# A fused RWKV layer on one core: powers of two 16x16 blocks streamed as 16 columns, with a new order of the engines' work

## The reference

```
def step(s, inp):
    q_, w_, k_, v_, a_, b_ = inp
    sa = jnp.einsum('bhij,bhj->bhi', s, a_)
    s = s * w_[:, :, None, :] + sa[..., None] * b_[:, :, None, :] + v_[..., None] * k_[:, :, None, :]
    return (s, jnp.einsum('bhij,bhj->bhi', s, q_))
...
_, y = jax.lax.scan(step, s0, (qt, wt, kt, vt, at, bt))
```

## Time and profile before

| | us |
|---|---|
| median of 3 runs | 3238.7 |
| lowest and highest | 3226.87, 3242.51 |
| the profiled execution | 3244.0 |
| its span, first to last instruction | 3242.2 |
| PE busy | 3029.1 (93%) |
| DVE busy | 2626.5 (81%) |
| ACT busy | 1974.8 (61%) |
| POOL busy | 1270.6 (39%) |

### The profile page before, as it was taken

How to read it: one execution, slowest core, us unless ns; L and a number is a source line. 1 busy time by engine, 2 the same in 40 slices (tenths; PEclk the granted TensorE clock), 3 DMA queues, 4 the chain that set the end, 5 groups by cost and what they waited for, 6 DMA issues and landing times.

```text
span 3242.2 us, 182735 instructions
## 1 busy us (share of the span) xinstructions
PE 3029.1 (93%) x84224; PEld 2675.6 (83%) x84224; DVE 2626.5 (81%) x5443; ACT 1974.8 (61%) x3519; POOL 1270.6 (39%) x1161
## 2 busy tenths in 40 slices
PE   6999999999999999999999999999999999999996
PEld 5888888888888888888888888888888888888884
DVE  4788888888888888887888888887888878888875
ACT  3575675665665665755656656656567566566563
POOL 4334334334334344343344343443433434433332
PEclk9999999999999999999999999999999999999998
DMA  3000000000000000000000000000000000000000
GB/s 118 10 23 20 17 23 19 18 20 18 22 20 17 23 20 17 23 20 17 22 20 19 20 17 23 20 17 23 20 17 23 20 17 20 20 20 20 16 17 19
DMA packets 39380, 70.47 MB, mean 22 GB/s; under 512 B 9812, under 2 KB 10836, under 8 KB 38616
## 3 DMA queue, kind: packets, MB, share of 16 engines
q1 hardware_dynamic: 38616, 58.77, 6.8%
HBM read 41.97 MB, written 16.78 MB: 18 GB/s over the span
## 4 chain that ended last, share of the span: by engine, by line
PE 92%; issue 3%; ACT 2%; DVE 2%; POOL 0%; POOLq 0%; ACTq 0%; DVEq 0%
PE bank L1070 30%; PE bank_a L1209 12%; PE bank L1273 8%; PE bank_a L1187 4%; PE bank L1077 4%; PE bank_b L1187 4%; PE bank_b L1244 3%; PE bank_b L1237 3%; PE bank_a L1237 3%; PE bank_a L1244 3%; PE bank_a L1217 2%; PE bank_a L1225 2%; PE bank L1123 2%; PE bank_a L1263 2%; PE bank_b L1263 2%
## 5 line engine op out<-in xcount | busy, mean ns | idle before, releaser
L504 ACT ACT_TABLE_LOAD x383 | 491.4, 1283 | 19.1 <-DVE shift L761 12.2
L1070 PE MATMUL bank<-xm_rg,w_r 128*128 128x128 f32 x2048 | 285.4, 282 | 4.3 <-issue 3.5
L504 ACT ACTIVATE u<-bank_a,parity 128x256 f32<-128x256 f32 x128 | 53.7, 471 | 386.7 <-PE bank_a L1253 386.7
L1209 PE MATMUL bank_a<-pw,w_ffn_int 32*32 32x64 f32 x16384 | 264.6, 216 | 22.0 <-issue 17.2
L1273 PE MATMUL bank<-w_o,yc 128*128 128x512 f32 x512 | 268.9, 626 | 11.0 <-DVE yc L744 9.3
L1209 PEld LDWEIGHTS bank_a<-pw,w_ffn_int 32*32 32x32 f32 x16384 | 239.6, 106 | 41.7 <-issue 21.3
L1070 PEld LDWEIGHTS bank<-xm_rg,w_r 128*128 128x128 f32 x2048 | 248.9, 191 | 26.8 <-issue 15.9
L504 ACT ACTIVATE u<-bank_b,parity 128x256 f32<-128x256 f32 x128 | 53.8, 471 | 342.3 <-PE bank_b L1253 342.3
L1070 PEld LDWEIGHTS bank<-xm_k,w_k 128*128 128x128 f32 x2048 | 241.2, 194 | 12.5 <-issue 3.8
L1070 PE MATMUL bank<-xm_v,w_v 128*128 128x128 f32 x2048 | 250.2, 275 | 0.0
L1070 PE MATMUL bank<-xm_k,w_k 128*128 128x128 f32 x2048 | 241.7, 277 | 3.5 <-issue 3.5
(11 more groups left out here) (204 smaller groups left out, 8540.4 us busy)
## 6 DMA issues: line engine op xcount, KB each, us to landing
xin<-in_x SPq DMA_DIRECT2D x128, 128.0 KB, 2.7
xres<-in_x SPq DMA_DIRECT2D x128, 128.0 KB
out<-o_sb SPq DMA_DIRECT2D x128, 128.0 KB, 2.4
w_ffn_int<-in_weight_q SPq DMA_DIRECT2D x1, 2048.0 KB, 10.8
w_k<-in_Wk SPq DMA_DIRECT2D x1, 1024.0 KB
w_r<-in_Wr SPq DMA_DIRECT2D x1, 1024.0 KB
w_v<-in_Wv SPq DMA_DIRECT2D x1, 1024.0 KB
w_o<-in_Wo SPq DMA_DIRECT2D x1, 1024.0 KB, 14.2
```

The source lines that it names most:

```text
L504: return nc.scalar.activation(out_, in_, func, **kw)
L1070: ins = mm(bank[:, o * n:(o + 1) * n], weights[:, k, o * P:(o + 1) * P], x[:, k].rearrange("p b t -> p (b t)"), start=(k == 0), stop=(k == ...
L1209: ins = mm(bank_a[q, 64 * n:64 * n + 64], pt[q, g, :], source[q, g, 0:2].rearrange("p j t -> p (j t)"), start=True, stop=True)
```

## The change

Four things are changed together.

1. The powers are streamed as 16 columns. Both 16x16 squares lie below each other in the 128 rows, so 16 columns hold them. Round 0 multiplies `pt` by 32 columns (16 of the first power, 16 of the first sum part), rounds 1 and 2 by 48 (16 of the power, 32 of the sums), in place of 64 each.
2. The block-diagonal form is no longer in PSUM. ACT writes it: two instructions copy the 16 columns into `spread`, one under the mask of the upper rows and one under that of the lower rows, and a third copies them to `pw`. DVE transposes `spread` from SBUF.
3. The first sum is made by POOL in a new function `first_sums`, two instructions of 256 columns. The identities that `first` held are gone. DVE adds 256 columns in round 0, where it added 512.
4. The calls are in another order on all four engines.

The core of the diff, with the calls of `tile_step` left out:

```diff
-        pw = sb("pw", [P, G, 2, CHUNK])
+        pw = sb("pw", [P, G, 3, HALF])
+        spread = sb("spread", [P, G, 2, HALF])
...
+            def first_sums(m):
+                pool.wait_ge(v_pm, count(m, 1, 1))
+                add(first[:, :, 1, 0:HALF], first[:, :, 0, 0:HALF], first[:, :, 0, HALF:]).then_inc(g_e, 1)
+                pool.wait_ge(g_e, count(m, 1, 1))
+                add(pw[:, :, 2, :], first[:, :, 1, 0:HALF],
+                    ident_half[:].unsqueeze(1).to_broadcast([P, G, HALF])).then_inc(g_ie, 1)
...
             def power(m, k):
                 act.wait_ge(p_pw, count(m, POWERS, k + 1))
-                run(pw[:, :, 0, :], pairs(bank_a)[:, :, 0, :], ACT.Copy).then_inc(a_pw, 1)
+                square = pairs(bank_a)[:, :, 0, 0:HALF]
+                act.wait_ge(v_ptT, count(m, POWERS + 1, k + 1))
+                run(spread[:, :, 0, :], square, ACT.Identity, scale=mask_half[:, 0:1])
+                run(spread[:, :, 1, :], square, ACT.Identity, scale=mask_half[:, HALF:HALF + 1]).then_inc(a_spread, 1)
+                run(pw[:, :, 0, :], square, ACT.Copy).then_inc(a_pw, 1)
...
             def power(m, k):
-                dve.wait_ge(p_pw, count(m, POWERS, k + 1))
+                dve.wait_ge(a_spread, count(m, POWERS, k + 1))
+                V.transpose(pt, spread[:].rearrange("p g a t -> p g (a t)")).then_inc(v_ptT, 1)
                 dve.wait_ge(a_pw, count(m, POWERS, k + 1))
-                V.transpose(pt, pairs(bank_a)[:, :, 0, :]).then_inc(v_ptT, 1)
-                before = first if k == 0 else pw
-                tt(pw[:, :, 1, :], pairs(bank_a)[:, :, 1, :], before[:, :, 1, :], ALU.add).then_inc(v_sums, 1)
+                if k == 0:
+                    tt(pw[:, :, 1, :], pairs(bank_a)[:, :, 0, HALF:], first[:, :, 1, HALF:], ALU.add).then_inc(v_sums, 1)
+                else:
+                    sums = pw[:, :, 1:3, :].rearrange("p g a t -> p g (a t)")
+                    tt(sums, bank_a[:].rearrange("p (g t) -> p g t", t=2 * CHUNK)[:, :, HALF:3 * HALF], sums,
+                       ALU.add).then_inc(v_sums, 1)
...
             def power(m, k):
                 if k == 0:
                     pe.wait_ge(v_e, count(m, 1, 1))
+                    pe.wait_ge(g_e, count(m, 1, 1))
...
-                    ins = mm(bank_a[q, 64 * n:64 * n + 64], pt[q, g, :],
-                             source[q, g, 0:2].rearrange("p j t -> p (j t)"), start=True, stop=True)
+                    if k == 0:
+                        ins = mm(bank_a[q, 64 * n:64 * n + CHUNK], pt[q, g, :], first[q, g, 1, :], start=True, stop=True)
+                    else:
+                        ins = mm(bank_a[q, 64 * n:64 * n + 3 * HALF], pt[q, g, :],
+                                 pw[q, g].rearrange("p a t -> p (a t)"), start=True, stop=True)
...
@@ DVE tile_step
+                if solve:
+                    token_major_values(m)
                 if mix:
                     norm_input(j)
```

More of the change, by code:

```diff
@@ L196, in rwkv_ffn_kernel @@
         a_pw, a_u, a_y, a_g, a_b2, a_k2, a_vT2 = (sem(f"a_{n}") for n in "pw u y g b2 k2 vT2".split())
-        g_qk, g_qkf, g_rkv = (sem(f"g_{n}") for n in "qk qkf rkv".split())
+        g_qk, g_qkf, g_rkv, g_e, g_ie = (sem(f"g_{n}") for n in "qk qkf rkv e ie".split())
+        a_spread = sem("a_spread")
         sold = sem("sold")
@@ L464, in tile_step @@
                     norm_rstd(j)
+                if solve:
+                    first_sums(m)
+                    decayed_state(m)
+                    bonus(m)
                 if project:
                     kept_keys(i)
-                if solve:
-                    decayed_state(m)
-                    bonus(m)
                 if finish:
@@ L981, in tile_step @@
                 if solve:
-                    token_major_values(m)
                     enter(m)
+                if finish:
+                    head_variance(n)
+                if solve:
                     power(m, 0)
[L985 to L989, removed]
                     token_major_keys(m)
@@ L995, in tile_step @@
                     scores_k(m)
+                if mix:
+                    norm_shift(j)
+                if project:
+                    decay_sums(i)
                 if finish:
                     gate_heads(n)
-                if project:
-                    decay_sums(i)
                 if solve:
@@ L1008, in tile_step @@
                     half_inverse(m)
-                    inverse(m)
                 if project:
@@ L1012, in tile_step @@
                 if solve:
+                    inverse(m)
                     right_hand_sides(m, 0)
@@ L1029, in tile_step @@
                     mixed_inputs(j, XK, XV)
+                    mixed_inputs(j, XRG, XRG)
                 if solve:
                     bonus(m)
-                if mix:
-                    mixed_inputs(j, XRG, XRG)
                 if project:
@@ L1216, in half_inverse @@
                 for n, g, q in ALL:
-                    ins = mm(bank_a[q, CHUNK * n:CHUNK * (n + 1)], pt[q, g, :], pw[q, g, 1, :], start=True, stop=True)
+                    ins = mm(bank_a[q, CHUNK * n:CHUNK * (n + 1)], pt[q, g, :],
+                             pw[q, g, 1:3].rearrange("p a t -> p (a t)"), start=True, stop=True)
                 ins.then_inc(p_t4, 1)
@@ L1224, in inverse @@
                 for n, g, q in ALL:
[L1225 removed]
+                    ins = mm(bank_a[q, HALF * n:HALF * (n + 1)], pt[q, g, :], pw[q, g, 2, :], start=True, stop=True)
                 ins.then_inc(p_t, 1)
```

75 lines of the change are left out of this document (34 added, 41 removed).

## The result

The changed kernel takes 3327.6 us (median; 3325.1 to 3328.9). The kernel before, run beside it, takes 3240.0 (3226.9 to 3242.5). The ratio is 1.029, 95% interval 1.027 to 1.031. I had forecast 3223 and a range up to 3262.

The account below looks back on a forecast made before the run. PE was taken as the bound (92% of the chain of waits). The mean tile, 48.15 + 1.76 - 1.05 + 0.2 = 49.06 us, was 0.24 less, 15 us over 63 tiles: 3223 us forecast, range 3185 to 3262.

Parts of the forecast that it names:

- PE's own work: PE's three powers rounds: narrower matmuls save 0.70 in round 0 and 0.45 each in rounds 1 and 2, 1.60 us a tile.
- Round 2 waits for ACT: At round 2 of the powers: ACT's longer copies make PE wait 0.8 us, leaving 0.36 of the 1.15 gained.
- The port: Ahead of `inverse`: POOL's `kmod` collides with DVE's `z`, `xx`, `mix` in SBUF, costing 1.05 us; gain of 0.8 becomes -0.24.
- Rival (a): At DVE's `z`, `xx`, `mix`: no collision with POOL's `kmod`; -0.65 us a tile, 3198 us; chance 0.25.
- Lo: At `mixed_inputs`: Tanh's table load and `lo` now follow the first `u`, so PE starts 0.37 us later in each tile.
- The gap-free tile: One tile without "issue" idle: 47.54 us before, plus 0.24 and 0.37, becomes 48.15.
- Gaps: "Issue" idle ahead of dense stages: 1.05 us a tile absorbed, 0.2 added by growth; mean tile 49.06 us against 49.30.
- Growth: Gaps ending at a fixed time grow when the stage before shortens: 0.38 us a tile, half of it free, so 0.2.
- Absorption: Gaps ahead of `inverse` fall into PE's waits: up to 1.83 us a tile free, 1.05 of 1.2 taken.
- Rival (b): Gaps not absorbed, perhaps lying in `inverse` or `from_state`, with the port's loss: 3290 us, 3257 at half absorption; chance 0.17.

Follow-up runs that it names:

- e4_width_bad: Kernel before with powers' matmuls only 32 and 48 columns wide (left-out sums not computed), block place fixed by a branch at slot 188: 3328.9 us, 1.030.
- e3_port: e3_after with GpSimd taking `kkp` ahead of `kmod`: 3154.7 us, 0.977 of the kernel before.
- e3_after: Changed kernel with a directive and branch fixing its block place at slot 220: 3196.5 us, 0.990 of the kernel before.
- e2_branch: Kernel before, each tile's keys put at slot 236 of a 256-instruction block, padding jumped over by a branch: 3152.0 us, 0.973.
- e4_width: e2_branch (slot 236) with powers' matmuls only 32 and 48 columns wide, left-out sums not computed: 3141.2 us, 0.972 of the kernel before.
- e1_width: Kernel before with only the powers' matmuls narrowed to 32 and 48 columns, left-out sums not computed: 3231.3 us, 0.999.
- e1_wait: Kernel before with one added PE wait, for DVE's `km` ahead of round 2, ready about when PE arrives: 3272.6 us, 1.012.
- e5_wait: e2_branch with the added wait of e1_wait ahead of round 2: 3247.5 us, 1.004 of the kernel before.
- e3_bad: e2_branch with slot 188 in place of 236: 3329.4 us, 1.031 of the kernel before.
- e5_behind: Kernel before with new powers, old engine order, branch at slot 220, and PE's last queries moved ahead of `from_values`: 3374.4 us, 1.044.

## Why the prediction was wrong

- *PE's own work, -1.60 us a tile.* Somewhat too large. A round of 128 records takes 1.56 us at 48 columns and 1.51 at 32 in PE's timeline, for 1.98 before; the sum is -1.3. Round 0 fell by 0.47 and not by 0.70: the 1.22 us of 32 columns came from `half_inverse` and did not hold there. The saving is worth nothing where a gap follows (`e4_width_bad`).
- *Round 2 waits for ACT.* The start is right: forecast at 13.98 us in the tile, seen at 13.94 in the gap-free tile. In part that is luck: PE waits there 0.33 us and not 0.8, since it comes 0.4 later by itself.
- *The port.* The mechanism was right and shows in `xx` (1.68 us for 0.69), and `inverse` starts at 25.48, forecast at 25.37. But on PE's path I had 1.05 us, and removing it gave 0.66 a tile (42 us / 63): without it I had `inverse` at 24.33, and in `e3_port` it starts at 24.88. Rival (a), no collision, is out.
- *Lo, 0.37.* The wait is 0.55, but taking it away brings 0.08 (5 us / 63), since DVE is the next to be late and the gaps grow.
- *The gap-free tile.* 48.15 forecast against 48.4 to 48.6. At fixed places the two kernels differ by 44 us, 0.7 a tile, and the forecast's terms make 0.6 of that. Some of this difference is gaps still: 0.56 us of them a tile in `e3_after`, 0.11 in `e2_branch`.
- *Gaps, -1.05 absorbed and +0.2 of growth.* **This step failed.** By the sum the mean tile was to be 0.91 us longer than the gap-free one; it is 2.2 longer (50.61 against 48.4). Three terms were wrong in it:
  - *Growth.* "Issue" idle rose by 1.37 us a tile (2.51 for 1.14) and not by 0.2. I multiplied the saving by the few stages that had a gap; but shorter stages get gaps where there were none (`e4_width`, 0.04 to 0.85 us behind round 2), and those that have one give nearly the whole saving back (`e4_width_bad`). Narrow matmuls alone bring 1.0 of it (`e1_width`), a wait just ahead of round 2 alone 0.3 (`e1_wait`).
  - *Absorption.* I had room for 1.83 us of gaps ahead of `inverse`. In the gap-free tile that starts at 434.0 PE's waits there are 0.33 at round 2, 0.31 for `mix` (rows below this list) and 0.12 at `inverse`, 0.76 in all. Over the middle tiles 0.13 of it is left, so some 0.6 us a tile was absorbed. The tile that starts at 276.9 shows it: gaps of 1.36, 1.51 and 1.22 us, and it is 3.31 longer than the gap-free one. What lies in `inverse` and behind it (43.7 us in all, 17.2 before) finds no wait to fall into. And a wait is not only room: just ahead of a dense stage it makes a gap (`e1_wait`, `e5_wait`).
  - *The clock* stood in the sum at nothing: an estimate of 25 us, 0.4 a tile.
- Rival (b), gaps not absorbed, had the right sign. Its mechanism is half right: the gaps in `inverse` and `from_state` were not absorbed, those ahead were in part, and what it lacks is the growth. I priced it at 3257 to 3290 and gave it 0.17; the time lies above that too.

The two waits of the gap-free tile at 434.0, in PE's timeline:

```profile
447.91 1.56 PE L1225 MATMUL bank_a<-pw,w_ffn_int 32*32 32x48 f32 x128 [0.33 <-DVE pw L751]
...
458.17 1.16 PE L1081 MATMUL bank<-mix,w_maa 128*128 128x128 f32 x8 [0.31 <-DVE mix L776]
```

The sum with measured times: gaps cost the kernel before 88 us (3240 - 3152), and the changed one at least 131 (3328 - 3196.5). So of the loss +44 us are tiles at a fixed place and +43 us gaps, the lower clock behind them included: at their fixed places neither kernel's clock falls in the middle of its trace. The fixed kernels ran on different chips; by their ratios to the kernel before it is 57 and 36 (0.9903 - 0.9726, and the rest of 0.0289, times 3240), and by the gap-free tiles, 48.41 and 47.54, it is 55 us for the tiles. The split is uncertain by some 10 us; that both parts are there is not. How the gaps' part divides further is not shown: the three terms above add up to more than it.

## What to carry to other kernels

Where idle is put down to "issue" ahead of dense stages, number the instructions and see whether the gaps return at multiples of 256. If they do, a faster dense stage is worth little until the boundaries have a good place, and that place (one directive with a branch, once per iteration) may be worth more than the change: here 2.7%, against -2.9% for a rewrite that takes 1.3 us of 49 off the busiest engine. Don't count a new wait ahead of such a stage as free because it is short. And price a long gap with the clock behind it.

## What the runs showed that I had not expected

- 160 empty instructions take 9.32 us on PE, 58 ns each, while 128 matmul records of `half_inverse` with their weight loads run in 1.22 us.
- A block boundary at a bad place costs PE 0.6 to 1.95 us of idle in the mean (`e3_bad`, `e5_behind`), and up to four of them fall in one tile (`e4_width_bad`).
- Behind a gap of 1.68 us PE was granted half of its clock (0.50), and the tile was 1.8 us longer than one with a gap of 1.69 us and the full clock.
- GpSimd's `kmod` keeps its 1.18 us in the median whether it collides with `xx` or not (`e3_after`, `e3_port`); it is DVE's instruction that is lengthened, by 1.0 us.
